# Attention kernel on one Trainium2 core: the stores of the result move from SyncE's queue to ScalarE's, three slots later

## The reference

```
x = x + gate(gn(x)) * gn(x)                  # one factor for each channel, from pooled values
x = x + attention(gn(x))                     # below
# attention: k, q = two 1x1 convolutions with norm and relu each (64 channels); v = 1x1 (64)
uk = concat([unfold3(keyf, d) for d in (1, 2, 4)])     # 27 neighbours of each pixel
sim = softmax(sum(uk * query[:, :, None], axis=1))
out = conv1x1(sum(sim * uv, axis=2), w_w, w_b)
```

## Time and profile before

| what | value |
|---|---|
| time, median of 3 runs | 1544.35 us (1541.41 to 1545.04) |
| profiled execution: its span | 1548.0 us, with no other time of it given |
| TensorE matmuls busy | 1471.3 us, 95% of the span |
| TensorE weight loads busy | 1197.9 us, 77% |
| VectorE busy | 1239.5 us, 80% |
| ScalarE busy | 1167.9 us, 75% |
| GpSimd busy | 776.4 us, 50% |
| DMA: read from HBM, written to it | 51.62 MB, 51.38 MB |
| store of one image, issue to landing (median) | 5.4 us |

### The profile page before, as it was taken

One profiled execution on the slowest core, in us unless ns is written; L12 is line 12 of the kernel. 1 busy time (PEld: TensorE's weight loads), 2 busy tenths in 40 slices (PEclk: granted clock), 3 DMA queues, 4 the chain that ended last, 5 costly groups with the idle time before them and its releaser, 6 DMA issues.

```text
span 1548.0 us, 35557 instructions
## 1 busy us (share of the span) xinstructions
PE 1471.3 (95%) x9287; PEld 1197.9 (77%) x9287; DVE 1239.5 (80%) x4629; ACT 1167.9 (75%) x3044; POOL 776.4 (50%) x2185
## 2 busy tenths in 40 slices
PE   2899999999999999999999999999999999999997
PEld 1687877788887887878788878888787887878886
DVE  6587878778887887888888888888787887888775
ACT  2687777778777777777777777777777777777876
POOL 6544455635465544455544455545455544455430
PEclk9999999999999999999999999999999999999999
DMA  3244454335453445553445553435453445553334
GB/s 131 60 135 120 148 163 125 129 103 162 148 163 109 135 113 150 157 159 116 135 114 156 154 162 114 138 107 163 148 162 107 136 114 151 157 149 120 95 76 138
DMA packets 104709, 205.99 MB, mean 133 GB/s; under 512 B 13632, under 2 KB 83776, under 8 KB 96448
## 3 DMA queue, kind: packets, MB, share of 16 engines
q1 hardware_dynamic: 103632, 203.49, 44.2%
q10 hardware_dynamic: 880, 0.23, 0.1%
HBM read 51.62 MB, written 51.38 MB: 67 GB/s over the span
## 4 chain that ended last, share of the span: by engine, by line
PE 76%; DVE 6%; issue 4%; ACT 4%; DMA 4%; POOL 3%; SPq 2%; ACTq 0%; DVEq 0%; POOLq 0%
PE ps_s L421 19%; PE ps_o L454 15%; PE ps_v L494 10%; PE ps_p L476 9%; PE ps_t L433 9%; PE ps_p L471 9%; DMA ksp<-kk 3%; PE ps_o L459 3%; DVE e L971 2%; DVE e L954 2%; ACT qq L624 1%; ACT eT L607 1%; ACT e L592 1%; SPq L366 1%; POOL g L767 1%
## 5 line engine op out<-in xcount | busy, mean ns | idle before, releaser
L592 ACT ACTIVATE e<-e,zmin 128x256 f32<-128x256 f32 x800 | 403.6, 505 | 192.0 <-DVE zmin L954 184.0
L954 DVE CUSTOM_DVE_ANT_0 e<-ps_s,mask 128x256 f32<-128x256 f32 x800 | 338.1, 423 | 139.6 <-PE ps_s L421 133.7
L454 PEld LDWEIGHTS ps_o<-eT,v 128*128 128x128 f32 x2688 | 380.8, 192 | 85.3 <-issue 81.5
L454 PE MATMUL ps_o<-eT,v 128*128 128x128 f32 x2688 | 434.0, 276 | 0.3 <-ACT eT L607 0.3
L421 PE MATMUL ps_s<-kk,qq 128*128 128x256 f32 x1408 | 428.3, 386 | 0.0
L433 PE MATMUL ps_t<-ident,e 128*128 128x128 f32 x1600 | 306.0, 273 | 0.2 <-DVE e L971 0.2
L607 ACT ACTIVATE eT<-ps_t 128x512 f32<-128x512 f32 (+1 forms) x416 | 235.5, 566 | 81.4 <-PE ps_t L433 79.8
L433 PEld LDWEIGHTS ps_t<-ident,e 128*128 128x128 f32 x1600 | 225.3, 141 | 81.2 <-DVE e L971 0.5
L421 PEld LDWEIGHTS ps_s<-kk,qq 128*128 128x128 f32 x1408 | 224.0, 192 | 47.2 <-issue 41.2
L971 DVE SCALAR_TENSOR_TENSOR e<-e,rz,keep 128x256 f32<-128x256 f32 x480 | 259.7, 541 | 0.1
L494 PE MATMUL ps_v<-wvox,xb 128*128 128x128 f32 x1600 | 219.9, 278 | 0.9 <-DVE v L992 0.8
(11 more groups left out here) (147 smaller groups left out, 1820.3 us busy)
## 6 DMA issues: line engine op xcount, KB each, us to landing
out_dram<-raw SPq DMA_DIRECT2D x32, 1568.0 KB, 5.4
raw<-in_x_dram SPq DMA_DIRECT2D x31, 1568.0 KB, 7.4
v<-v SPq DMA_DIRECT2D x192, 224.0 KB, 3.0
kk<-kk SPq DMA_DIRECT2D x192, 112.0 KB, 2.2
ksp<-kk SPq DMA_DIRECT2D x192, 64.0 KB, 2.4
v<-v_last SPq DMA_DIRECT2D x64, 128.0 KB, 2.9
kk<-kk SPq DMA_DIRECT2D x32, 224.0 KB, 2.9
v<-v_last SPq DMA_DIRECT2D x64, 96.0 KB, 2.7
```

The costliest lines, as they stand in the source:

```text
L454: last = nc.tensor.matmul(o[:, UPIX * (u - 1):UPIX * (u + 1)], v[:, s, u, :], eT[:, UPIX * (base + 2 * u - 1):UPIX * (base + 2 * u + 1)], ...
L592: nc.scalar.activation(e[:, i, :], e[:, i, :], ACT.Exp, bias=zmin[:, i:i + 1], scale=-1.0, accum_out=zs[:, i:i + 1]).then_inc(e_done.next( ...
L954: nc.vector.tensor_tensor_reduce(e[:, i, :], ps_s[(TILES * n.parity() + t) % 2][:, 0:KEYS], mask[:].rearrange("p s h a b -> p (s h a b)"), ...
```

## The change

The `store` of an image is taken from SyncE's program and put into ScalarE's, with the same wait and the same transfer. It no longer stands in slot 5 of the next image but at the start of slot 8 (`STORE`), ahead of that slot's `eT` copy; the last image's store stands in slot 6 of the drain. SyncE waits at the end for the full count of `stored`, since it no longer counts these transfers itself.

```diff
 LOAD = 15
+STORE = 8
...
-                    def store(m):
-                        sp.wait_ge(o_done.sem, o_done.count(m, STRIPS))
-                        sp.dma_start(out[m.index(), :, :],
-                                     raw[:, m.offset % RAWS, :]
-                                     ).then_inc(stored[m.parity()].next(16), 16)
...
                     def slot(n, t):
                         if t == LOAD and (n + 3).exists():
                             load(n + 3)
-                        m, k = lagged(n, t, FINAL)
-                        if k == TILES - 1 and m.exists():
-                            store(m)
...
-                    for transfers in x_in + stored + k_copied + [v_copied]:
+                    for transfers in x_in + k_copied + [v_copied]:
                         sp.wait_ge(transfers.sem, transfers.here)
+                    for transfers in stored:
+                        sp.wait_ge(transfers.sem, transfers.per * (NIMG // 2))
...
+                    def store(m):
+                        act.wait_ge(o_done.sem, o_done.count(m, STRIPS))
+                        act.dma_start(out[m.index(), :, :],
+                                      raw[:, m.offset % RAWS, :]
+                                      ).then_inc(stored[m.parity()].next(16), 16)
...
                     def slot(n, t):
+                        if t == (STORE if n.exists() else FINAL) and (n + -1).exists():
+                            store(n + -1)
                         m, k = lagged(n, t, TRANSPOSE)
                         if m.exists() and (k % 2 == 1 or k == TILES - 1):
                             copy(m, k // 2)
```

## The result

| | before | after |
|---|---|---|
| median of 4 runs | 1542.97 us (1541.41 to 1545.04) | 1681.51 us (1674.91 to 1685.03) |
| span of the profiled execution | 1548.0 us | 1679.3 us |
| mean granted TensorE clock in it | 0.997 | 0.970 |

The ratio is 1.0893, with a 95% interval of 1.0867 to 1.0918. The direction was forecast, the size was not: 1583 was predicted, with 1522 to 1605 as the range.

The account below looks back on a forecast made before the run. TensorE was taken as the bound, waiting for `ksp` copies. Span 1548.0 − 20.5 (late copies now) + 59 (1.9 us of lateness in 31 images) = 1586.5; as a median 1583 us, range 1522 to 1605.

Parts of the forecast that it names:

- The bound and the cause of the present waits: TensorE is the bound; late `ksp` copies of block 4 cost it 20.5 us, the most the change can give.
- When ScalarE issues the store: Slot 8, right behind `zmin` of slot 7: about 2.4 us after the old store issue, 0.2 before the first `ksp` copy.
- Rival A: Store comes behind block 4's `ksp` copies, or engines let small packets through; all 20.5 us come back: 1524; chance 0.33.
- The order on the DMA engines: The store takes the engines before block 4's `ksp` copies; the second copy ends behind it either way.
- The landing: Second `ksp` copy of block 4 lands 8.0 to 8.95 us after the old store issue; 8.5 taken, 6.57 harmless.
- 31 x 1.9 = 59 us: Lateness of the second `ksp` copy, 1.9 us in each of 31 images; bounds 44 and 84 us.
- My own signs: Second `ksp` copy landing 4.7 to 5.7 us after issue, TensorE waiting in all 31 images, periods of 47.5 to 48.5.
- The held issue: SyncE's second `ksp` issue, held 0.7 us behind the full queue before; if again, landing at +8.95.
- rival C: Second `ksp` issue held until the store is through (+7.3), landing at +9.3 to 9.6: 1614; chance 0.06.
- What follows on SyncE: `v` and block 5 copies share engines with the store until about +7.3; block 5 needed some 7 us after issue: nothing.
- ScalarE's own cost: 31 more issues of 0.35 to 0.60 us on ScalarE, in sequencer time before the slot 8 `eT` copy: nothing.
- Rival B: No change: store still first, copies behind; only SyncE's 0.35 us of issue time moves, off the path: 1544; chance 0.08.

Follow-up runs that it names:

- e9: Kernel before with SyncE's store moved to slot 13, behind the block 6 copies, and the load from slot 15 to 16: 1531.63 us, ratio 0.9919.
- e10: The change with ScalarE's store still in slot 8 but behind the `eT` copy instead of ahead of it: 1571.37 us, ratio 1.0192.
- e3: Kernel before with the store, still on SyncE, issued between `kk` and the first `ksp` copy of block 4: 1636.13 us, ratio 1.0596.
- e8: The change with only half of each image's pixels stored, in as many packets of half the size: 1564.32 us, ratio 1.0114.
- e5: The change with ScalarE's store in slot 6 instead of slot 8, about the issue time of the kernel before: 1542.93 us, ratio 0.9988.
- e1: The change with ScalarE's store one slot later, in slot 9: 1591.28 us, ratio 1.0297.
- e6: Kernel before with SyncE's store moved to slot 8, behind that slot's two `v` copies: 1534.35 us, ratio 0.9924.
- e2: Kernel before with the store kept on SyncE but moved to the start of slot 8: 1575.81 us, ratio 1.0199.
- e7: The change with ScalarE's store in slot 10 instead of slot 8: 1543.29 us, ratio 0.9979.
- e4: The change with 12 filler matmuls on TensorE ahead of its wait for the `ksp` copy of tile 10: 1643.78 us, ratio 1.0637.

## Why the prediction was wrong in size

- **The bound and the cause of the present waits**: right. `ksp` copies of block 4 behind the store were what TensorE waited for, and the earlier trace rows gave 20.5 us as the most there is. e9 gives back 12.4 us by the medians of its set of runs (1544.03 before, 1531.63), and 18.9 us by the spans of the two profiled executions (1548.0, 1529.1).
- **When ScalarE issues the store**: right. Forecast at +2.4, 0.04 us behind `zmin`; measured 0.04. e10 shows the same rule at another place. Rival A, that the datapath is waited for, falls.
- **The order on the DMA engines**: right in the main. In the change and in e3 the second `ksp` copy lands 0.9 us or more behind the store's last packet in every image, and half a store makes it earlier (e8). At the end the two overlap: the first packets of `ksp` start 4.9 us behind the store's issue, the store's last packet ends at 6.3.
- **The landing, +8.0 to +8.95, middle +8.5: this step failed, in one term, the end of the store.** In the image shown the second `ksp` copy lands at 775.91 + 6.6 = 782.5. The store's issue was at +2.4 by my own count (0.04 us behind `zmin` in both traces), so this is +9.9; over the 31 images it is +10.1 on average. The term 31 x 1.9 = 59 us should have been 31 x 3.5 = 109. My own signs missed it too: 4.7 to 5.7 us from issue to landing (6.6), periods of 47.5 to 48.5 (49.2 to 53.4). I had let the store end 4.6 us after its issue, as in the earlier trace rows, or up to 0.3 later, and had added 1.65 us at most for the copy behind it. The packets of the traces say which of the two was off (us behind the store's issue, medians of 31 images):

| kernel | store's first packet | its last packet ends | from first to last | second `ksp` copy lands behind that |
|---|---|---|---|---|
| before | 0.85 | 4.96 | 4.1 | 1.4 |
| e5, ScalarE, 2 us ahead of the copies | 0.84 | 4.92 | 4.1 | 1.6 |
| e3, SyncE, behind `kk` | 1.14 | 5.30 | 4.2 | 1.1 |
| the change | 1.35 | 6.26 | 4.9 | 1.2 |

What comes behind the store is as before; the store itself ends 1.3 us later. The change's queues from 779.9 to 781.3, 4.9 to 6.3 us behind the issue, where the store of before has ended:

```profile
q1 hardware_dynamic: 271, 0.18, 47.7%
q10 hardware_dynamic: 30, 0.18, 39.1%
```

Of the 1.3 us, 0.5 are a later first packet, with the packets of `kk` on the engines at that time, and 0.8 are a longer store. From its first to its last packet the store takes 4.9 us here and 5.5 in e1, with copies of the other queue beside it, but 5.0 also in e6, in one queue right behind two `v` copies. It takes 4.1 to 4.3 in the kernel before, e2, e3, e5 and e7. So the traffic on the engines as the store starts goes with its length; how much of the 0.8 is the second queue's stays open.
- **The held issue and rival C**: the issue of the second copy took 1.57 us where I counted 0.7, but that is not what made it late. It was over at 777.48, 2.5 us behind the store's issue and 3.8 before the store's last packet ended. Rival C let the issue wait until the store is through (+7.3; it was over at +4.9) and so came to a landing of +9.3 to 9.6. That this is near +9.9 is luck. Its time, 1614, has no term for the clock either.
- **The clock: left out of the sum.** One fall, costing 1.6 us, was in the rows of before, behind a wait of 1.9 us. I forecast longer waits in every image and still carried no term for it. e4 measures 37 us.
- **The sum as it should read**, in spans: 1548.0 − 20.5 + lateness + clock = 1679.3. The clock is 1679.3 − 1642.0 = 37.3 (e4), so the lateness is 114.5, or 3.7 us an image with the instruction fetches in it, for which I had 59. The span that my sum gave was 1586.5: of the 92.8 us between, 55.5 are lateness that my landing did not have and 37.3 the clock. Of the 114.5, 109 are the landing at tile 10, and the rest I can't place. In medians the gap is 98.5, since the profiled execution of the kernel before was longer than all four of its runs, which that of the change was not.
- **"What follows on SyncE: nothing"**: wrong, and hidden in the change itself. There SyncE waits 2.9 us in each image for the `v` copies too, but TensorE is held up at tile 10 before that. In e1 and e2 it decides: SyncE's wait for the `v` copies, six issues, then the keys of block 6. I had counted when each late copy is needed by TensorE, and not what stands behind SyncE's wait for it. So rival A's 1524 was also wrong for a store that just clears the `ksp` copies; the store in slot 9 gives 1591.
- **ScalarE's own cost, nothing**: right. In e5 it has all the issues and the time of before.
- **Rival B, that only issue time changes hands**: right where the order stays (e5), not where the slot moves it. The Trainium skill (DMA: Bandwidth & Descriptors, "Issuing engines are not separate DMA queues") says that issuing from several engines saves only issue time; e5 agrees, with a ratio to the kernel before of 0.9988 (0.9972 to 1.0004). The change costs more than issue time, but there the store has moved among the copies too.

## What to carry to other kernels

Here a 1568 KB transfer held back every 64 KB copy that reached the engines after it, whichever queue either was in. Put such a transfer where the next copies are not needed for as long as it takes, and read from the trace when it is really issued, which for the DMAs on ScalarE here was when the instruction ahead had its wait met (the change and e10). When a queue waits for a copy that has become late, count what stands behind that wait in its program, not only who reads the copy. And where TensorE is the bound, a wait of some microseconds is paid a second time in clock: if it repeats, price it from a row at the lower level. And where other copies are on the engines as the large transfer starts, do not take its end from a row in which it starts alone: here it moved from 5.0 to 6.3 us behind the issue.

## What was unexpected of the hardware

- A store issued on ScalarE's queue 0.27 us before a 64 KB copy of SyncE's had the engines to itself for 2.5 us (87 packets against 7 small ones), and the copy landed after 6.2 us, the one behind it after 6.6, instead of 2.0.
- The issue of a DMA is held by a large transfer in another queue too: 1.33 us instead of 0.62 for the first `ksp` copy in e5, 1.57 for the second in the change.
- Behind idle waits of about 3 us the granted clock fell to 0.50 for over 3 us in 26 of 31 images; behind those of e3, 2.5 us on average, in 14; behind those of e8, 0.9 us on average, in 2. The same wait filled with matmuls left it at 0.998.
